# Attention, routing and experts on one core: the reciprocal of the denominators moves one step later in VectorE's order

## What is computed

```python
S = jnp.einsum('chlm,chld->chmd', k_phi, v)
sum_k = jnp.sum(k_phi, axis=2)
numer = jnp.einsum('chlm,chmd->chld', q_phi, S)
denom = jnp.maximum(jnp.einsum('chlm,chm->chl', q_phi, sum_k), EPS)
out_heads = numer / denom[..., None]
...
return out @ w_out.T
...
x = x + _layernorm(_L0_attn_ref(...))
```

## Time and profile before

| | |
|---|---|
| runs | 2134.17, 2136.22, 2138.1 us (median 2136.22) |
| span of the profiled execution | 2130.7 us; its own time is not listed beside it. The median of the runs lies 5.5 us above the span |
| busy | PE 86%, DVE 57%, ACT 53%, POOL 36% of the span |
| in 984 to 1326.5 us (steady part of the stage) | PE 289.4, DVE 287.8, POOL 256.7, ACT 256.3 us busy of 342.5 |

### The profile page before, as it was taken

The page is one execution under the profiler, slowest core; times in us unless marked ns, Lnnn a source line. Parts: engine busy times, 40 slices in busy tenths (PEclk is TensorE's granted clock), DMA queues, the critical chain, the costliest instruction groups (busy, mean ns, idle before and its releaser), DMA issues.

```text
span 2130.7 us, 33664 instructions
## 1 busy us (share of the span) xinstructions
PE 1825.4 (86%) x12931; PEld 890.0 (42%) x12976; DVE 1207.3 (57%) x2230; ACT 1124.4 (53%) x1371; POOL 768.8 (36%) x718
## 2 busy tenths in 40 slices
PE   8899999999978999699788887635998899997785
PEld 6444444444436788133233333312444444443332
DVE  7676667666650000158788888872444434445786
ACT  5554554555525666478677877422444444442343
POOL 0000000000000000024677788876677777761110
PEclk9999999999998999899999999857999999999997
DMA  7435353445328887568678765443789999987983
GB/s 255 150 116 197 105 182 131 149 164 183 121 97 213 209 214 191 132 166 230 186 241 234 227 206 193 159 183 100 164 194 222 244 232 243 220 150 231 330 301 138
DMA packets 188848, 405.15 MB, mean 190 GB/s; under 512 B 33812, under 2 KB 72084, under 8 KB 172064
## 3 DMA queue, kind: packets, MB, share of 16 engines
q1 hardware_dynamic: 83184, 222.41, 35.2%
q10 hardware_dynamic: 68640, 124.26, 16.7%
q0 software_dynamic: 36864, 56.32, 14.2%
HBM read 237.06 MB, written 177.08 MB: 194 GB/s over the span
## 4 chain that ended last, share of the span: by engine, by line
DVE 14%; PE 14%; DMA 10%; issue 8%; POOL 8%; ACT 4%; SPq 1%; POOLq 0%; DVEq 0%; ACTq 0%
POOL slot_dram L1260 4%; PE s_gates L1485 4%; PE s_ups L1485 3%; DMA s_rows<-rows_dram,s_slot 3%; PE s_ys L1500 3%; DMA acc_dram<-s_y,s_slot 3%; DMA s_spread<-share_dram 2%; ACT s_xT L1531 2%; PE s_turned L1462 1%; DMA den_dram<-s_den 1%; DVE s_heads L1101 1%; DVE s_stats L1651 1%; DVE s_x L1670 1%; POOL acc_dram L1426 1%; DMA s_dens<-den_dram 1%
## 5 line engine op out<-in xcount | busy, mean ns | idle before, releaser
L258 PE MATMUL s_proj<-s_xT,keep_wqkv 128*128 128x512 f16 x1536 | 341.8, 380 | 0.0
L1260 POOL DMA_INDIRECT slot_dram<-keep_filled,keep_slots x256 | 301.7, 1179 | 95.2 <-issue 73.8
L1426 POOL DMA_INDIRECT acc_dram<-s_y,s_slot x128 | 203.0, 1586 | 93.5 <-issue 34.2
L898 PE MATMUL s_y<-keep_wo,s_at_hl 128*128 128x512 f16 x768 | 191.0, 402 | 44.9 <-ACT s_z L988 44.8
L258 PEld LDWEIGHTS s_proj<-s_xT,keep_wqkv 128*128 128x128 f16 x1536 | 147.6, 98 | 183.4 <-issue 12.6
L237 PE MATMUL s_proj<-keep_wqkv,s_xT 128*128 128x512 f16 x768 | 179.5, 393 | 34.5 <-ACT s_xT L500 34.5
L1540 ACT ACTIVATE s_gate<-s_gates 128x512 f32<-128x512 f32 x96 | 57.1, 597 | 262.5 <-PE s_ups L1485 217.0
L339 POOL TENSOR_SCALAR s_rstd<-s_mv 128x4 f32<-128x4 f32 x16 | 16.0, 998 | 494.8 <-DVE s_mv L354 494.8
L1610 DVE SCALAR_TENSOR_TENSOR s_h<-s_gate,s_ups 128x512 f32<-128x512 f32 x96 | 65.9, 687 | 213.2 <-ACT s_gate L1540 213.1
L518 ACT ACTIVATE s_hl<-s_rot 128x1024 f16<-128x1024 f32 x64 | 67.6, 1057 | 221.0 <-DVE s_rot L400 220.5
L676 ACT ACTIVATE s_phi<-s_logits 128x1024 f32<-128x1024 f32 x128 | 131.0, 1023 | 85.1 <-PE s_logits L697 85.1
(11 more groups left out here) (165 smaller groups left out, 3207.4 us busy)
## 6 DMA issues: line engine op xcount, KB each, us to landing
s_x<-x_in SPq DMA_DIRECT2D x32, 1024.0 KB, 9.7
qk_dram<-s_hl ACTq DMA_DIRECT2D x32, 1024.0 KB, 5.9
keep_ahead<-qk_dram SPq DMA_DIRECT2D x48, 512.0 KB
acc_dram<-s_zero SPq DMA_DIRECT2D x17, 1024.0 KB, 11.5
v_dram<-s_v ACTq DMA_DIRECT2D x16, 1056.0 KB
s_v<-v_dram SPq DMA_DIRECT2D x16, 1056.0 KB, 10.8
s_spread<-share_dram SPq DMA_DIRECT2D x64, 256.0 KB
x_dram<-s_x ACTq DMA_DIRECT2D x16, 1024.0 KB, 5.2
```

Of the source, the lines that this page charges most:

```text
L258: mm = nc.tensor.matmul(out[:, 512 * b:512 * b + 512], left, right, start=(c == 0 and i == 0), stop=(c == EC - 1 and i == 2))
L898: mm = nc.tensor.matmul(y[m % 2][:], at_hl[n % 2][:, s, c, a * P:(a + 1) * P], keep["wo"][:, w, c, :], start=(c == 0 and i == 0), stop=(c ...
L1260: nc.gpsimd.indirect_dma_start(out=io["slot"], out_offset=bass.IndirectOffsetOnAxis(ap=slots[n % 2][:, a * K + j:a * K + j + 1], axis=0), ...
L1426: nc.gpsimd.indirect_dma_start(out=io["acc"], out_offset=bass.IndirectOffsetOnAxis(ap=slot[e % RING][:, a, 0:1], axis=0), in_=y[e % 2][:, ...
```

## The change

`make_share` runs one step later: for group n at step 4n + 5 rather than 4n + 4, and within the step between `measure_x1` and `aggregate` rather than after `aggregate`. Nothing else changes; PE, ACT, POOL and SP run the same lists.

```diff
@@ -1218,11 +1218,11 @@
                     measure_y(s - MEASURE)
                 if 0 <= s - ADD < NT:
                     measure_x1(s - ADD)
+                n = group_at(s, A + 1)
+                if n is not None:
+                    make_share(n)
                 if 0 <= s - MEASURE < UNITS:
                     aggregate(s - MEASURE)
-                n = group_at(s, A)
-                if n is not None:
-                    make_share(n)
                 n = group_at(s, A + 2)
                 if n is not None:
                     divide(n)
```

## The result

The changed kernel takes **2178.94 us** (median of 4 runs, 2173.94 to 2188.9), the kernel before 2135.19 us beside it. The ratio is 1.0199, with a 95% interval of 1.0173 to 1.0226: slower by some 43 us, where the prediction had 2164 us, 28 us slower, and a range of 2140 to 2186. The direction and the mechanism were right; one term of the sum was far too small, and the time lies above the likeliest band of 2150 to 2175.

A forecast was written before the change was run, and what follows sets the result against it. DVE's waits were taken to bound the kernel, chiefly for `dens`. Lateness less slack 12.9, filling pipeline 5.9 and collision 8.8 sum to 27.6 us on the 2130.7 span; with 5.5 from span to median, 2164 us, range 2140 to 2186.

The forecast's parts named there:

- Lateness of the reciprocal: At step 1 the reciprocal waits for ACT's high half, coming 4.2 us after the aggregation; 20.9 us net in 12 groups.
- the straggler: The one group of 13 whose wait for `dens` at the end of step 0 was 10.8 us.
- The wait for `dens` goes, the wait for `spread` takes its place: On DVE, 40.3 us of `dens` waits nearly vanish; `divide` waits 2 to 4 us in nearly every group instead.
- POOL's wait for the slots: A sign in the profile after: on POOL this wait would be longer; no size given.
- The filling pipeline: In groups 1 to 3 the reciprocal comes another 1.9, 2.0 and 2.0 us later: 5.9 us.
- The collision: ACT's 1 MB rows store meets the spread loads: 1.1 us in eight groups, 8.8 us; bounds 0 and 31 us.
- slack: Time from reciprocal to `divide` above 8.47 us in nine groups without a printed wait: 8.0 us, taken off the 20.9.
- rival C: The 10.8 us `dens` wait and late spread landings were accidents and need not recur: 2139 us, no tellable change; chance 0.10.
- Rival B: ACT's rows store runs ahead of the spread loads and takes its whole price: 50 us, 2186 us; chance 0.17.
- Rival D: At `divide`, data lands within about 7.2 us of the reciprocal, so no wait: 19 us less, 2118 us; chance 0.06.
- Rival E: The delay is swallowed behind `divide` by PE's or POOL's own waits: 5 to 10 us slower, 2144 us; chance 0.12.
- the rule weighed in the prediction: A DMA takes about 2.0 us plus bytes over 436 GB/s: `share` store and spread loads 6.5 us, against 8.47 traced.

The follow-up runs named there:

- the dose run: The kernel before with the reciprocal in step 1 directly behind `make_low`: 2141.48 us, ratio 1.0048.

## Why the prediction came out as it did

I compare the 13 groups from 3 to 15 of the two profiles.

- *Lateness of the reciprocal.* Predicted 4.2 us after the aggregation, measured 4.20 to 4.26 in ten of twelve groups (4.93 in one where `rstd` was late, 6.20 in group 3, predicted 6.2). In the 12 groups without the straggler it comes later by 24.1 us in sum, against 20.9 + 2.0. Right, and choosing the high half over the slower `rstd` was too.
- *The wait for `dens` goes, the wait for `spread` takes its place.* Right: 40.3 to 9.0 and 5.5 to 64.5 us. The single waits are 4.3 to 6.3 us in groups 6 to 15, where 2 to 4 were named as a sign, and the cycle is 34.7 us, not 31.5 to 33. One sign was wrong: POOL's wait for the slots did not grow but fell, from 16.4 to 6.0 us over the 11 cycles; POOL waits for the aggregation instead, 56.9 us and not 15.5.
- *The filling pipeline.* The reciprocal of groups 1 and 2 comes 1.85 and 2.03 us later; 1.9 and 2.0 were predicted.
- *The collision* is the term that was mis-sized. I took 1.1 us in eight groups, 8.8 us, with an upper bound of 2.4 us in 13. In groups 6 to 15 the time from reciprocal to `divide` is 10.6 to 12.7 us, 11.7 on average: 3.2 us above the floor of 8.47, more than the bound. Summed over the 13 groups it grew by 20.1 us where slack and collision together were to give 8.8 - 8.0, under 1 us. I had taken one pair of points (1.1 us for 1.4 us of lead lost), and for the bound a line through it, though the lead went to nothing. The store was not 0.6 us ahead of the loads either: in groups 6 to 14 it was issued between 0.3 us ahead of the first load and 0.5 us behind it. The groups of all eleven profiles, from group 3 on, in which `divide` waited show that it isn't a line. From the first spread load to `divide` it is 6.7 to 8.2 us where the rows store is issued 1.4 to 3.1 us behind the loads (11 cases), 9.1 to 11.5 where it is issued within 0.6 us of them on either side (19 cases), and 6.6 to 7.7 where it is issued over 4 us ahead (4 cases). So the price belongs to transfers that start together, not to their order; no run has the store between 0.7 and 4 us ahead of the loads.
- *A second collision.* In group 15 of the changed kernel the loads took the usual 7.0 us, and all that is lost was lost in the `share` store, issued 0.42 us behind the rows store and landed after 4.05 us instead of 1.47:

```profile
1379.65 0.37 ACTq L1027 DMA_DIRECT2D rows_dram<-s_hl  x1
1380.07 0.34 SPq L840 DMA_DIRECT2D share_dram<-s_share  x1
1384.12 1.71 SPq L845 DMA_DIRECT2D s_spread<-share_dram  x4
```

- *Stragglers* (rival C). The late group 5 came back and grew: 8.98 us of wait on top of 5.0 us already covered, its reciprocal 3.2 us later than before. It stands in every run, at the same group, with 3.8 to 12.6 us of wait. It was no accident, and C was wrong in that.
- *Rival B* had the right two transfers at too small a price: it comes to 2186 only by being charged in all 13 groups, and a store 0.5 us behind the loads costs as much as one 0.3 us ahead. The measured 2179 lies nearer to its 2186 than to the 2164 of the sum, and it was B's end that made the range wide enough. *Rival D* is what happens once `divide` is covered, but this kernel doesn't cover it. *Rival E* had a small part, 4.5 us in three groups, of which 2.6 us are in group 11, whose wait for `rstd` of 2.5 us vanished.

The sum by the profile: 24.1 (lateness) + 20.1 (landing) + 3.2 (straggler) + 3.9 - 0.4 (groups 1 and 2) - 4.5 (behind `divide`, in groups 1, 2 and 11) comes to 46 us. From the first `read_total` to the last `divide` it is 508.8 us instead of 463.0. The stages behind differ by 8 us between the two profiled executions (788 and 796 us from the last `divide` to the end), and the start by 2.6 us. Over all kernels here the stages behind take 782 to 796 us, so nothing ties the 8 us to the change.

Of the rule weighed in the prediction: by the Trainium skill, "DMA: Bandwidth & Descriptors", "Anatomy of one DMA", store and loads would, as an estimate, have landed in 6.5 us. In the changed kernel and the nine experiments no `divide` that waited found its data under 7.9 us after the reciprocal. The measurement stands; the fit is for GpSimd's path. By its parts it is the loads that are off: 6.6 us at least where 4.4 were estimated, while the store of 32 KB took 1.5 and not 2.1.

What stays open: why group 5 waits 3.8 to 12.6 us for `dens` in each kernel (in the kernel before, ACT's x1 store, issued 3.8 us ahead of the den store, took 14.4 us to land there and 5.1 in group 4, so both queues were held up), and whether a transfer behind a large one waits for its completion or for bandwidth.

## What to carry to other kernels

A wait that disappears from an engine's list is a gain only if the operation behind it is not the head of a chain: here the reciprocal heads a chain of five DMAs over DRAM, and each microsecond that it waits less on VectorE by coming later is paid where the chain ends. Measure the whole chain, find how much other work lies ahead of its end, and move the end (with all that hangs on it, on every engine) together with the head: here the head alone cost 43 us, the end alone 7, and both together gained 7. And when a transfer moves, look at what the other queues issue within 2 us of it: the price of two that start together is not read off from two that nearly did.

## What the runs showed of the hardware

- A 32 KB store took 4.9 us rather than 1.5 when 1 MB had been issued 1.3 us ahead of it on another engine's queue. Loads of 1 MB took some 3 us more on average when a store of 1 MB was issued within 0.6 us of them (groups 6 to 14 of the changed kernel, 10.1 us from the first load to `divide`, against 7.0 in group 10 of the kernel before), next to nothing more with 2.3 us between (7.2 in group 9 of the dose run), and nothing more with the store 4.5 us ahead (7.0 in group 15 of the changed kernel).
- Moving either 1 MB store by a step made the kernel before slower (1.0059 and 1.0107). DMA is busy 0.73 of the stretch there; neither of the two places tried was free, other places were not tried.
